# Two routed-mixture stages of a 12-stage kernel: half of the shared expert's work moved from ahead of the row gathers to behind the expert loop

## The chip, the cores and the metric

One core of a Trainium2 chip runs the whole kernel in one launch. The metric is the device time of that launch in microseconds (us), the median over several runs; smaller is better. The engines are TensorE (PE in the profile; PEld are its weight loads), VectorE (DVE), ScalarE (ACT), GpSimd (POOL) and SyncE (SP, which issues most of the DMAs).

## What is computed

Twelve residual stages over 1024 tokens of width 256, `x = x + f(layernorm(x))`, some with a factor of 0.5: routed mixtures, retention, a binarized layer, attention, two kinds of state-space mixers. The change touches the last layer's feed-forward part only, which runs twice, ahead of and behind that layer's mixer (stages 9 and 11 of 0 to 11):

```python
scores = jax.nn.sigmoid(xt @ gate_w.T)                       # 1024 tokens, 8 experts
top_scores, top_idx = jax.lax.top_k(scores, 2)
top_scores = top_scores / (jnp.sum(top_scores, axis=-1, keepdims=True) + 1e-20) * 2.5
combine = jnp.sum(jax.nn.one_hot(top_idx, 8) * top_scores[..., None], axis=1)
h = jnp.einsum('td,edh->eth', xt, w1)                        # d = 256, h = 176
u = jnp.einsum('td,edh->eth', xt, w3)
y = jnp.einsum('eth,ehd->etd', jax.nn.silu(h) * u, w2)
routed = jnp.einsum('etd,te->td', y, combine)
shared = jax.nn.silu(xt @ sw1) * (xt @ sw3) @ sw2            # the shared expert
x = x + 0.5 * (routed + shared)                              # xt = layernorm(x)
```

## The kernel before

The program is written engine by engine. For each stage a planner function makes one list of steps, and every engine's code walks the same list and issues its own part of each step in that order; semaphores do the rest. For these stages the planner is `moe3_order` (L639), and the walkers are `pe_moe3` (TensorE), `a_moe3` (ScalarE), `v_moe3` (VectorE), `g_moe3` (GpSimd) and `sp_moe3` (SyncE). So the list is at once the order of five queues. A step that an engine has nothing to do for is skipped by it.

The steps of the list before, in order:

- `gate`: ScalarE's sigmoid of the eight logits per token (they came from the last `route` step of the stage before, `a_route`), then VectorE picks the two largest (`v_gate3`) and leaves a 0/1 mask.
- `up 0 (0, 1)`, `up 0 (2)`, `up 1 (0, 1, 2)`: the shared expert's gate and up products in plain fp32 (`pe_up3`), half 0 for tokens 0 to 511 and half 1 for tokens 512 to 1023, each in three blocks of rows (0, 1, 2) and each block four matmul records.
- `count`: TensorE counts with a triangular matrix, from the mask, at which place in its expert's list each token stands; VectorE turns the count into one-hot codes (`v_count3`), ScalarE multiplies these by the token numbers (`place`, eight small instructions).
- `table`: eight matmuls make from the codes the table of tokens by expert and place; VectorE spreads it (`v_table3`), and `slots` (two matmuls and a cast) makes the indices for the gathers. GpSimd then gathers the rows of experts 0 to 2 from `Hd`, the normalized tokens in DRAM, 128 rows in one indirect DMA and three of these for an expert (`g_rows3`), and at step `in 0` those of expert 3.
- `swiglu 0`, `swiglu 1`: VectorE multiplies silu and up of each half.
- `split`: ScalarE copies the weights of experts 0 and 1 into rounded high parts (four copies); `low 0` is VectorE's subtraction that leaves the low part of expert 0's gate and up weights. The routed products run as three fp32r passes, high by high, high by low and low by high.
- `overflow`: a branch on all engines that is taken only if an expert has more than 384 tokens; with this input it isn't. Behind it all engines meet at a small DMA (`joined`).
- `down 0` to `down 3`, `sum 0` to `sum 3`: the shared down products, two tiles of 128 tokens each, and their addition to the residual `X` on VectorE.
- the loop over the 8 experts as a software pipeline of three steps, newest first: `in` (transposes of the gathered rows, high and low parts), `mid` (gate, up, silu), `out` (down products, copy, store of the rows to `ye` in DRAM). So a turn is `in e+2`, `mid e+1`, `out e`. `codes` and `weights` compute on VectorE where each token's two results lie and with which weights they count.
- `fetch t 1`, eight times: GpSimd gathers for each tile of 128 tokens the row of the lower of its two experts (0 to 6), which waits until expert 6's rows are stored; then `fetch t 0`, eight times, which waits for expert 7's.
- `add t 1`, then `add t 0` on VectorE: `X` plus weight times fetched row; behind each `add t 0` come the layernorm and transposes for the next stage, or, in stage 11, the store of the output.

The weights of an expert lie in one of five lanes of the buffer `ering` (L2269):

```python
        def lane(e):
            return (0, 1, 2, 3, 4, 0, 1, 2)[e]
```

In stage 9 lane 4 first holds the shared expert's weights, so that expert 4's are loaded behind `down 3`; in stage 11 the shared weights lie elsewhere, and all five lanes are loaded at the start of the stage, in order.

## Time and profile before

| | |
|---|---|
| median of 3 runs | 1900.29 us (1895.18 to 1905.56) |
| the profiled execution | 1914.95 us |
| its span in the profile | 1913.1 us |
| mean granted TensorE clock in it | 0.902 of 2.4 GHz |
| busy: TensorE, VectorE, ScalarE, GpSimd | 83%, 75%, 60%, 47% of the span |
| stage 9 in the trace | about 1088 to 1198 us |
| stage 11 in the trace | about 1803 to 1913 us |

The profile is of one execution; its times are from the span's start. Where two rows carry the same number of matmuls, a plain fp32 matmul counts as two records (it runs in two passes). A row of a timeline merges neighbours of the same kind: `1088.50 5.37 PE ... x8` is eight records that together last 5.37 us. `<-` names what ended the engine's idle time before a row; `remote` and `another core or an unknown queue` stand where no recorded event fits.

### The profile page before, as it was taken

How to read it: one execution, taken by the hardware profiler on the slowest of the kernel's cores; microseconds unless marked ns; L12 is line 12 of the kernel's file. 1: busy time of each engine (PE TensorE's matmuls, PEld its weight loads, DVE VectorE, ACT ScalarE, POOL GpSimd, SP SyncE). 2: the span in 40 equal slices, each digit the busy share in tenths (PEclk: the TensorE clock that was granted, in tenths of full speed). 3: DMA queues.
4: the chain of work that ended last, by engine and by line, in shares of the span. 5: the costliest groups of instructions: out<-in, count | busy, mean ns of one | idle time of the engine just before them, and what ended most of it. 6: DMA issues, size and time to landing. Idle time of an engine off the chain costs nothing.

```text
span 1913.1 us, 28345 instructions
## 1 busy us (share of the span) xinstructions
PE 1585.1 (83%) x10286; PEld 1286.8 (67%) x10286; DVE 1428.8 (75%) x2995; ACT 1154.6 (60%) x2381; POOL 900.9 (47%) x914
## 2 busy tenths in 40 slices
PE   6899468978997276789888975889999999999874
PEld 4799346875996145578567774577777777777573
DVE  6788668657886576777786766778888888888764
ACT  4588146644883137831882243688888888888542
POOL 0677432003775610030252053157787787878353
PEclk9999788988998577979997987899999999999887
DMA  8698310513994200000003042001001000000243
GB/s 306 211 290 261 94 42 25 179 41 98 283 290 148 81 24 1 1 1 1 1 1 115 21 136 95 9 15 34 17 20 31 20 20 28 23 12 15 91 132 108
DMA packets 87449, 158.88 MB, mean 83 GB/s; under 512 B 13560, under 2 KB 62840, under 8 KB 86264
## 3 DMA queue, kind: packets, MB, share of 16 engines
q1 hardware_dynamic: 72696, 116.96, 18.6%
q0 software_dynamic: 14592, 39.87, 7.3%
q8 instruction: 89, 1.46, 0.3%
q14 instruction: 72, 0.59, 0.1%
HBM read 124.28 MB, written 32.51 MB: 82 GB/s over the span
## 4 chain that ended last, share of the span: by engine, by line
PE 29%; DVE 12%; POOL 7%; ACT 4%; issue 3%; DMA 1%; another core or an unknown queue 0%; POOLq 0%; DVEq 0%; ACTq 0%
PE ps L79 26%; POOL work L91 3%; DVE work L91 3%; DVE wt L99 3%; PE ps L83 2%; ACT wt L87 2%; DVE ering L91 2%; POOL work_r L91 1%; ACT L87 1%; DVE X L99 1%; DVE wt L91 1%; POOL wt_r L91 1%; POOL H L145 1%; DVE H L95 1%; ACT work L87 1%
## 5 line engine op out<-in xcount | busy, mean ns | idle before, releaser
L79 PE MATMUL ps<-work_r 128*128 128x256 f32 (+2 forms) x1200 | 243.9, 294 | 8.0 <-DVE work_r L91 3.3
L79 PE MATMUL ps<-wt,work 128*128 128x256 f32 (+1 forms) x1176 | 235.7, 374 | 13.4 <-ACT work L87 8.7
L145 POOL DMA_INDIRECT work<-Hd,work x176 | 169.6, 964 | 137.1 <-DVE work L111 88.9
L79 PE MATMUL ps<-H_r,wt_r 128*128 128x512 f32 x576 | 223.2, 432 | 9.7 <-POOL wt_r L91 7.5
L87 ACT ACTIVATE work<-ps 128x512 f32<-128x512 f32 (+5 forms) x339 | 152.0, 478 | 126.1 <-PE ps L79 59.4
L79 PEld LDWEIGHTS ps<-wt,work 128*128 128x128 f32 (+1 forms) x1176 | 183.1, 203 | 44.2 <-ACT work L87 9.5
L79 PEld LDWEIGHTS ps<-work_r 128*128 128x128 f32 (+1 forms) x1200 | 190.2, 188 | 24.0 <-DVE work_r L91 14.0
L99 DVE SCALAR_TENSOR_TENSOR wt<-ps,wt 128x511 f32<-128x511 f32 (+2 forms) x234 | 174.4, 747 | 22.4 <-ACT wt L87 16.5
L87 ACT ACT_TABLE_LOAD x113 | 145.0, 1283 | 41.3 <-DVE lmv L119 23.5
L91 DVE TENSOR_TENSOR work<-work,ps 48x256 f32<-48x256 f32 (+3 forms) x242 | 128.1, 530 | 50.5 <-PE ps L79 37.5
L91 POOL TENSOR_TENSOR work<-work 128x256 f32<-128x256 f32 (+2 forms) x164 | 162.2, 997 | 6.6 <-ACT work L87 1.3
L91 POOL TENSOR_TENSOR work<-work,wt 128x512 f32<-128x512 f32 x72 | 88.5, 1230 | 133.4 <-DVE work L91 126.5
L79 PEld LDWEIGHTS ps<-H_r,wt_r 128*128 128x128 f32 x576 | 109.3, 190 | 59.1 <-POOL wt_r L91 12.4
L79 PE MATMUL ps<-work_r,ering_r 128*128 128x256 f32 (+3 forms) x480 | 142.6, 297 | 0.0
L79 PE MATMUL ps<-ering,wt 128*64 128x128 f32 (+3 forms) x1488 | 108.7, 286 | 38.7 <-DVE wt L91 25.1
L87 ACT ACTIVATE wt<-wt 128x512 f32<-128x512 f32 (+3 forms) x153 | 132.6, 932 | 5.4 <-DVE wt L91 4.2
L79 PE MATMUL ps<-wt,hT 128*128 128x8 f32 (+4 forms) x384 | 110.3, 432 | 30.1 <-DVE hT L111 14.7
L87 ACT ACTIVATE lrs<-lmv,epsc 128x1 f32<-128x1 f32 x96 | 28.0, 296 | 173.9 <-DVE lmv L119 136.8
L79 PEld LDWEIGHTS ps<-ering,wt 128*64 128x64 f32 (+2 forms) x1488 | 85.1, 137 | 64.8 <-DVE wt L91 27.5
L145 POOL DMA_INDIRECT ering<-ye,get x80 | 78.6, 983 | 104.0 <-DVE X L99 84.3
L91 DVE TENSOR_TENSOR ering<-ering 128x1024 f32<-128x1024 f32 (+4 forms) x88 | 125.8, 1429 | 0.5
L79 PE MATMUL ps<-ering_r,work_r 128*128 128x256 f32 (+1 forms) x398 | 124.5, 348 | 0.4 <-ACT work L87 0.4
(249 smaller groups left out, 4211.3 us busy)
## 6 DMA issues: line engine op xcount, KB each, us to landing
ering<-in_moe_w SPq DMA_DIRECT2D x87, 624.0 KB, 4.9
ye<-work SPq DMA_DIRECT2D x64, 256.0 KB
wt<-in_ssd_wg SPq DMA_DIRECT2D x64, 128.0 KB, 2.2
ye<-work SPq DMA_DIRECT2D x16, 384.0 KB
Hd<-H SPq DMA_DIRECT2D x32, 128.0 KB, 1.7
ye<-early SPq DMA_DIRECT2D x1, 4096.0 KB, 14.6
wt<-in_ssd_wg SPq DMA_DIRECT2D x8, 512.0 KB, 3.6
work<-Hd,work POOLq DMA_INDIRECT x176
```

Of the source, the lines that this page charges most:

```text
L79: self.last = self.e.matmul(o, l, r, start=start, stop=stop, skip_group_check=True)
L83: self.last = self.e.transpose(o, a, ident)
L87: self.last = self.e.activation(o, a, f, **kw)
L91: self.last = self.e.tensor_tensor(o, a, b, op)
L95: self.last = self.e.tensor_scalar(o, a, s1, s2, op0, **(dict(kw, op1=op1) if op1 is not None else kw))
L99: self.last = self.e.scalar_tensor_tensor(out=o, in0=a, scalar=s, in1=b, op0=op0, op1=op1, **kw)
L145: self.last = self.e.indirect_dma_start(out=out, out_offset=at(out_off), in_=in_, in_offset=at(in_off))
```

## The change

It does these things, in the list of steps and what follows from it:

- `split` goes to the front, right behind `gate`; `count` goes ahead of blocks 1 and 2 of `up 0`; `low 0` goes ahead of `table`. `up 1`, `swiglu 1` and all of the `down` and `sum` steps leave the head.
- Behind `overflow` VectorE makes the low parts of expert 0's down and of expert 1's weights.
- The loop is written out: a turn is `in e`, `mid e-1`, `out e-2`. Its end becomes: `down 0`, `out 6`, the eight `fetch t 1`, `mid 7`, `sum 0`, `up 1 (0, 1)`, `out 7`, `up 1 (2)`, `down 1`, `swiglu 1`, the eight `fetch t 0`, `sum 1`, `down 2`, `down 3`, `add` of tiles 0 to 3 from the first fetches, `sum 2`, `sum 3`, `add` of tiles 4 to 7 from the first fetches, then `add t 0` as before.
- ScalarE computes one throw-away sigmoid ahead of the last logits' copy.
- Stage 9 uses four lanes for experts, stage 11 five; the wait for `down 3` and the load behind it are gone. The shared expert's two halves use the same two silu buffers.

```diff
@@ -638,28 +638,25 @@
 
         def moe3_order(si):
             todo, begun, end = [], set(), Steps()
-            todo += [("gate",), ("up", 0, (0, 1)), ("count",), ("up", 0, (2,)), ("place",), ("up", 1, (0, 1, 2)), ("table",)]
-            todo += [("slots",), ("swiglu", 0), ("swiglu", 1), ("split",), ("overflow",), ("low", 0)]
-            todo += [("down", g) for g in range(4)] + [("sum", g) for g in range(4)]
-
-            def expert(e):
+            todo += [("gate",), ("split",), ("up", 0, (0,)), ("count",), ("up", 0, (1, 2)), ("place",), ("low", 0), ("table",)]
+            todo += [("slots",), ("swiglu", 0), ("overflow",)]
+
+            for e in range(8):
                 todo.append(("in", e))
-                if e == 1:
-                    todo.append(("codes",))
-                elif e == 2:
-                    todo.append(("weights",))
-                elif e == 7:
-                    todo.extend(("fetch", t, 1) for t in range(NT))
-                yield
-                todo.append(("mid", e))
-                yield
-                todo.append(("out", e))
-
-            pipeline([expert(e) for e in range(8)], 3, 1, True)
-            for t in range(NT):
-                todo.append(("fetch", t, 0))
-            for t in range(NT):
-                todo.append(("add", t, 1))
+                if e in (1, 2):
+                    todo.append(("codes",) if e == 1 else ("weights",))
+                if e >= 1:
+                    todo.append(("mid", e - 1))
+                if e >= 2:
+                    todo.append(("out", e - 2))
+            todo += [("down", 0), ("out", 6)]
+            todo.extend(("fetch", t, 1) for t in range(NT))
+            todo += [("mid", 7), ("sum", 0), ("up", 1, (0, 1)), ("out", 7), ("up", 1, (2,)), ("down", 1), ("swiglu", 1)]
+            todo.extend(("fetch", t, 0) for t in range(NT))
+            todo += [("sum", 1), ("down", 2), ("down", 3)]
+            todo += [("add", t, 1) for t in range(HALF)]
+            todo += [("sum", 2), ("sum", 3)]
+            todo += [("add", t, 1) for t in range(HALF, NT)]
             for t in range(NT):
                 todo.append(("add", t, 0))
                 end.live.append(after(todo, si, t, begun))
@@ -2091,6 +2088,8 @@
 
         def a_route(a, si, t):
             b = ps.of("route", si, t)
+            if t == NT - 1 and STAGES[si] == "moe3":
+                a.act(lrs[:, 0, 0:1], epsc[:, 0:1], ACT.Sigmoid)
             a.wait_ge(PE, "route", si, t)
             a.act(logits[:, t, :], b.ap[:, 0:8], ACT.Copy).then_inc(A, "logits", si, t).frees(b)
 
@@ -2266,8 +2265,11 @@
                 return SSD["ssd3"].xz.rearrange("p c n -> p (c n)")[:, 0:WP]
             return ering[:, 4, :]
 
-        def lane(e):
-            return (0, 1, 2, 3, 4, 0, 1, 2)[e]
+        def lanes(si):
+            return 5 if STAGES[si - 1] == "ssd3" else 4
+
+        def lane(si, e):
+            return e % lanes(si)
 
         def pe_up3(pe, si, h, blocks):
             wgu, cs = gate_up(shared_weights(si)[:, 0:GU]), slice(h * 512, h * 512 + 512)
@@ -2331,12 +2333,12 @@
                     hi, lo = m.xT[e % 2]
                     pe.wait_ge(V, "xl", si, e)
                     pe.wait_ge(V, "gu", si, e)
-                    w = (m.wgr[e % 2], ering[:, lane(e), 0:GU])
+                    w = (m.wgr[e % 2], ering[:, lane(si, e), 0:GU])
                     pe_swiglu(pe, (si, e), gate_up(w), lambda c, cs: (hi[:, c, :], lo[:, c, :]), slice(0, MAIN3))
                     pe.mark("up", si, e)
                 elif s[0] == "out":
                     e = s[1]
-                    w = down_rows((m.wdr[e % 3], ering[:, lane(e), GU:WP]))
+                    w = down_rows((m.wdr[e % 3], ering[:, lane(si, e), GU:WP]))
                     for j in range(NB):
                         if j % 2 == 0:
                             b = ps.take(pe, "y", si, e, j // 2)
@@ -2350,16 +2352,16 @@
 
         def a_weights3(a, si, e, part):
             h, cut = (M5.wgr[e % 2], slice(0, GU)) if part == "gu" else (M5.wdr[e % 3], slice(GU, WP))
-            a.wait_ge(esem[lane(e)], si, e)
+            a.wait_ge(esem[lane(si, e)], si, e)
             if part == "gu" and e >= 2:
                 a.wait_ge(PE, "up", si, e - 2)
             if part == "dn" and e >= 3:
                 a.wait_ge(PE, "out", si, e - 3)
-            a.act(rnd(h), ering[:, lane(e), cut], ACT.Copy).then_inc(A, part, si, e)
+            a.act(rnd(h), ering[:, lane(si, e), cut], ACT.Copy).then_inc(A, part, si, e)
 
         def low_weights3(q, si, e, part):
             h, cut = (M5.wgr[e % 2], slice(0, GU)) if part == "gu" else (M5.wdr[e % 3], slice(GU, WP))
-            w = ering[:, lane(e), cut]
+            w = ering[:, lane(si, e), cut]
             q.wait_ge(A, part, si, e)
             q.tt(rnd(w), w, f32(h), ALU.subtract).then_inc(q.done, part, si, e)
 
@@ -2378,7 +2380,9 @@
                         a.act(x, x, ACT.Copy, scale=m.ids[:, t:t + 1]).then_inc(A, "numbered", si, t)
                 elif s[0] == "up" and s[2][-1] == 2:
                     h = s[1]
-                    a_swiglu(a, (si, 8, h), m.sg[2 * h], m.sg[2 * h + 1], 512)
+                    if h:
+                        a.wait_ge(V, "sw", 0, si, 6)
+                    a_swiglu(a, (si, 8, h), m.sg[0], m.sg[1], 512)
                 elif s[0] == "split":
                     for e in range(2):
                         a_weights3(a, si, e, "gu")
@@ -2403,8 +2407,8 @@
                     hi, lo = m.aT[e % 2]
                     if e >= 2:
                         a.wait_ge(V, "sw", 0, si, e - 2)
-                    else:
-                        a.wait_ge(V, "sw", 0, si, 8, e)
+                    elif e == 0:
+                        a.wait_ge(V, "sw", 0, si, 8, 0)
                     a_swiglu(a, (si, e), m.sg[2 * e % 4], m.sg[(2 * e + 1) % 4], MAIN3)
                     a.wait_ge(V, "sw", 1, si, e)
                     a.act(rnd(hi[0:48, 1, :]), lo[0:48, 1, :], ACT.Copy).then_inc(A, "ah", 1, si, e)
@@ -2524,7 +2528,7 @@
                 elif s[0] == "swiglu":
                     h = s[1]
                     v.wait_ge(G, "zero rows", si)
-                    v_swiglu(v, (si, 8, h), m.aD, slice(h * 512, h * 512 + 512), m.sg[2 * h], m.sg[2 * h + 1])
+                    v_swiglu(v, (si, 8, h), m.aD, slice(h * 512, h * 512 + 512), m.sg[0], m.sg[1])
                 elif s[0] == "sum":
                     g = s[1]
                     b = ps.of("down", si, 8, g)
@@ -2541,6 +2545,8 @@
                     v.mark("routed", si)
                     v_overflow3(v, si)
                     v.wait_ge(s_join, "in", si)
+                    for e, part in ((0, "dn"), (1, "gu"), (1, "dn")):
+                        low_weights3(v, si, e, part)
                 elif s[0] == "codes":
                     v_codes3(v, si)
                 elif s[0] == "weights":
@@ -2548,16 +2554,13 @@
                 elif s[0] == "in":
                     e = s[1]
                     hi, lo = m.xT[e % 2]
-                    if e:
+                    if e >= 2:
                         low_weights3(v, si, e, "gu")
-                    if e >= 2:
                         v.wait_ge(PE, "up", si, e - 2)
                     for c in range(2):
                         b = ps.of("x", si, e, c)
                         v.wait_ge(A, "xh", si, e, c)
                         v.tt(rnd(lo[:, c, :]), b.ap[:, 0:MAIN3], f32(hi[:, c, :]), ALU.subtract).then_inc(V, "xl", si, e).frees(b)
-                    if e < 2:
-                        low_weights3(v, si, e, "dn")
                 elif s[0] == "mid":
                     e = s[1]
                     hi, lo = m.aT[e % 2]
@@ -2737,7 +2740,7 @@
             if e == 8:
                 sp.dma(shared_weights(si), D["moe3_w"][8]).then_inc(s_shared3, si, by=16)
             else:
-                sp.dma(ering[:, lane(e), :], D["moe3_w"][e]).then_inc(esem[lane(e)], si, e, by=16)
+                sp.dma(ering[:, lane(si, e), :], D["moe3_w"][e]).then_inc(esem[lane(si, e)], si, e, by=16)
 
         def sp_moe3(sp, si):
             m = M5
@@ -2766,14 +2769,11 @@
                 if s[0] == "overflow":
                     sp_overflow3(sp, si)
                     sp.dma(joined, zero[0:1, 0:1]).then_inc(s_join, "in", si, by=16)
-                    if before:
-                        sp.wait_ge(PE, "down", si, 8, 3)
-                        sp_expert3(sp, si, 4)
                 elif s[0] == "out":
                     e = s[1]
-                    if e + 5 < 8:
+                    if e + lanes(si) < 8:
                         sp.wait_ge(PE, "out", si, e)
-                        sp_expert3(sp, si, e + 5)
+                        sp_expert3(sp, si, e + lanes(si))
                     sp.wait_ge(V if e % 2 else A, "y", si, e)
                     rows = ye[e * ROOM:e * ROOM + MAIN3, :].rearrange("(j p) d -> p j d", p=128)
                     sp.dma(rows, m.yo[e % 2]).then_inc(s_ye[e % 2], "out", si, e, by=16)
```

## Rows read from the trace of the kernel before

**Rows 1.** Windows of stages 9 and 11: busy us (count) per engine, granted clock, DMA share, GB/s.
```profile
1104.45:1123.21 18.76, 10.94 (x45) 9.12 (x45) 7.45 (x16) 1.63 (x4) 12.53 (x14) 0.81 0.36 94
1123.21:1168.60 45.39, 45.30 (x300) 44.74 (x300) 38.12 (x81) 31.24 (x66) 17.50 (x17) 0.97 0.46 147
...
1820.20:1839.01 18.81, 11.19 (x45) 9.27 (x45) 7.42 (x16) 1.63 (x4) 12.52 (x14) 0.82 0.32 87
...
1884.60:1909.38 24.78, 0.01 (x1) 0.00 (x0) 8.29 (x18) 0.00 (x0) 15.18 (x16) 0.55 0.49 143
```

**Rows 2.** Timeline of stage 9's head: start us, us, instruction xcount [idle before <-releaser].
```profile
1088.47 1.28 ACT L87 ACT_TABLE_LOAD   x1
...
1088.50 5.37 PE L79 MATMUL ps<-hT,ering 128*128 128x512 f32 x8 [0.32 <-PE ps L79]
...
1089.76 0.26 ACT L87 ACTIVATE work<-logits 128x64 f32<-128x64 f32 x1
...
1092.22 0.30 DVE L95 TENSOR_SCALAR work<-work 128x64 bf16<-128x64 f32 x2
...
1093.70 0.55 PE L79 MATMUL ps<-work,triB 128*128 128x64 bf16 x16
...
1096.43 2.46 ACT L87 ACTIVATE work<-work 128x128 f16<-128x128 f16 x8 [1.94 <-DVE work L91]
...
1099.03 0.15 DVE L111 CAST over<-most 128x1 uint32<-128x1 f32 x1
...
1102.14 0.42 DVE L91 TENSOR_TENSOR work<-ps,work 128x256 f32<-128x256 f32 x1 [2.95 <-PE ps L79]
```

**Rows 3.** Timeline of stage 9's first gathers and shared down products.
```profile
1104.45 0.99 POOL L145 DMA_INDIRECT work<-Hd,work  x1 [14.19 <-DVE work L111]
...
1107.45 0.92 DVE L91 TENSOR_TENSOR ering_r<-ering,wt_r 128x736 fp32r<-128x736 f32 x1 [0.39 <-issue]
1107.47 9.63 PE L79 MATMUL ps<-ering,work 128*128 128x256 f32 x32 [3.50 <-DVE work L91]
...
1118.29 0.95 POOL L145 DMA_INDIRECT work<-Hd,work  x1 [0.31 <-issue]
```

**Rows 4.** Chain that ended last, in stage 9's head: start us, us, what.
```profile
1116.16 5.28 another core or an unknown queue
```

**Rows 5.** DMA of 1104.4 to 1113.3 us: gathers' queue, packets, MB, share.
```profile
q0 software_dynamic: 288, 0.79, 31.2%
```

**Rows 6.** Timeline of stage 11's head.
```profile
1815.79 2.55 ACT L87 ACTIVATE wt_r<-ering 128x736 fp32r<-128x736 f32 x4
...
1823.79 9.88 PE L79 MATMUL ps<-wt,work 128*128 128x256 f32 x32 [4.08 <-DVE ering_r L91]
...
1837.27 0.76 DVE L99 SCALAR_TENSOR_TENSOR X<-ps,X 128x256 f32<-128x256 f32 x2 [4.21 <-remote]
```

**Rows 7.** DMA of 1803 to 1808.9 us: queue of the weights, packets, MB, share.
```profile
q1 hardware_dynamic: 481, 1.56, 74.9%
```

**Rows 8.** Timeline of stage 9's tail.
```profile
1161.36 0.51 PE L79 MATMUL ps<-work_r,wt_r 128*128 128x384 f32 x2
...
1164.50 0.28 PE L79 MATMUL ps<-wt_r 128*128 128x256 f32 x1
...
1170.18 0.96 POOL L145 DMA_INDIRECT H<-ye,get  x1 [9.89 <-DMA ye<-work]
...
1183.00 0.48 DVE L99 SCALAR_TENSOR_TENSOR X<-work,wk,X 128x256 f32<-128x256 f32 x1 [0.77 <-DMA work<-ye,get]
```

**Rows 9.** Timeline behind the last expert of stage 0.
```profile
195.23 3.62 PE L79 MATMUL ps<-ering,wt 128*128 128x256 f32 x16
...
198.68 5.31 PE L79 MATMUL ps<-hT,ering 128*128 128x512 f32 x12
...
211.97 0.59 ACT L87 ACTIVATE work<-ps 48x512 f32<-48x512 f32 x1 [3.67 <-remote]
```

**Rows 10.** Timeline of GpSimd where gathers run beside VectorE's subtractions.
```profile
1124.31 1.13 POOL L145 DMA_INDIRECT work<-Hd,work  x1 [0.30 <-issue]
```

## Prediction

> **What bounds the kernel now.** First the windows, because the shares of a 1913 us span say nothing of a change that touches two of twelve stages. Stage 9 and stage 11 (the routed mixtures of the last layer) have the same four stretches, and two of them leave TensorE idle [rows 1]. From the first row gather to the first routed matmul it works 10.94 of 18.76 us in stage 9 (11.19 of 18.81 in stage 11); through the experts 45.30 of 45.39; behind the last expert 0.01 of 24.78 in stage 11. So the stage is: a head that leads to the gathers' indices, a run of gathers, a loop that TensorE bounds, and a tail that waits for GpSimd's gathers and VectorE's additions. Only head and tail can give.
>
> Then the head in order of time [rows 2]. The sigmoid of the gate waits for its table (load of 1.28 us, sigmoid 0.01 us behind it). TensorE meanwhile runs eight fp32 matmuls, at 0.67 us each, up to 1093.87; only then comes the count, though the mask was there by 1092.5. VectorE's table starts 8.44 us behind the count's start, the first gather 2.31 us behind that.
>
> Then the run of gathers [rows 3]: twelve, one each 1.25 us, from 1104.45 to 1118.29. The shared down products (9.63 us) run beside them and end at 1117.10. But their last sum has to wait: the chain that ended last has 5.28 us of "another core or an unknown queue" from 1116.16 to 1121.44 ahead of it [rows 4]. Stage 11 repeats it, 4.21 us of idle ahead of the same sum [rows 6]. Counted from the end of the down records this is 4.34 us in stage 9 and, with down records that end at 1833.67, 3.6 us in stage 11. 1121.44 is also 3.15 us behind the last gather's issue: either a plain wait, or TensorE's results come late while gathers run. This is the open question of the case.
>
> **The change, part by part.**
>
> *Sigmoid table ahead.* The dummy sigmoid stands before the last logits' copy, where ScalarE was idle, so the mask comes 1.28 us sooner, at 1091.2 [rows 2]. The Trainium skill (ScalarE: Activation LUTs, What ACT_TABLE_LOAD costs) adds a drain of about 1.38 us to each load; by that the step would bring 1.4 us more. The row shows the sigmoid right behind the load, so I don't count it.
>
> *Count behind one block.* Four of the eight matmuls now lie ahead of it: 1088.50 + half of 5.37, rounded up to 3.44 because the first ones run at the half clock (0.86 each) = 1091.94 instead of 1093.70. Gain 1.76; the mask no longer holds it.
>
> *Second up half away from the table.* Between count and table stood 16 matmuls, now 8, and the table waits for ScalarE's numbering instead. VectorE's work behind the count is about 5.5 us, then the low part of expert 0's weights (0.92 to 0.98 us [rows 3]), so the table starts near 1091.94 + 5.5 + 0.98 = 1098.4 instead of 1102.14: −3.7 us in stage 9. In stage 11 the four weight copies (0.64 us each [rows 6]), now ahead of the silus and the numbering, need expert 1's weights. Two experts and the shared constants, 1.56 MB, have arrived only at 1808.9 [rows 7]. From there: copies of expert 1, 1.3, plus the second of expert 0, 0.64; silu's table load 1.28; two silus at 0.59 [rows 9] and numbering 2.46 [rows 2]; together 6.9 with the gaps, so the table starts near 1815.9 to 1816.1 instead of 1817.89 (2.31 ahead of the first gather at 1820.20 [rows 1]): −1.85 us. If those weights come 1.5 us later, nearly nothing is left of this one.
>
> *Gathers to the first expert.* The first routed up product waits for experts 0's and 1's rows, because expert 1's transposes stand ahead of it on TensorE. Six gathers (0.79 MB) had landed 8.85 us behind the first issue [rows 5]. Six transposes (0.12 each), copy, subtraction and hand-overs make 10.3 us from first gather to first routed matmul. Before it was 18.76 and 18.81 in the profile [rows 1]; without the unnamed 4.34 and 3.6 us it would be 14.4 and 15.2. So the gain is 8.4 us in both (8.46, 8.51) if the unnamed stall is in timed runs too, and 4.1 and 4.9 us if it is not. The same 10.3 rests on TensorE's results coming promptly beside the rest of the gathers; if they come only once the twelfth has landed, the gain is nought. These are the two bounds. I take the lower gain, 4.1 and 4.9, since the profiled execution (1914.95 us, span 1913.1) lies 14.7 us above the median of the timed runs, and a stall of this kind, repeated in stages 0, 2, 9 and 11, could be part of that.
>
> *Clock.* TensorE now idles longer ahead of the first expert, and restarts at 1.2 GHz: 0.86 us instead of 0.43 for four or so large matmuls is 1.7 us; before also restarted after some idling. Between 0 and 1.7, I take +0.8 in each stage.
>
> *VectorE beside gathers.* Three subtractions (0.92 each) replace idling, and hold nothing: the first expert's rows land 8.85 us behind. Where gathers met such work they took 1.13 us, against 0.95 [rows 10]: under 1 us for all three, left in the range. The Trainium skill (SBUF — State Buffer, Who interferes with whom) has a VectorE instruction with two SBUF inputs exclude GpSimd's reads for its whole length. By that each gather could start 0.9 later, 2.8 us in a stage, 5.5 in all, and the time would be about 1891.
>
> *Expert loads.* Four lanes instead of five in stage 9: expert 4's 0.64 MB load behind expert 0's end, in less than the 5.9 us that 1.56 MB took [rows 7], and are split an expert's 5.66 us (45.30 / 8 [rows 1]) or more later. Hidden, at most +0.3. SyncE's queue loses a wait and gains none. The overflow branch keeps its place beside the gathers.
>
> *Tail* [rows 8]. Expert 7's up products (1161.36 to 1164.50, 3.14) now stand behind expert 6's end, and one down group ahead of it: a group is 8 of the 16 matmuls that take 3.62 [rows 9], so 1.81. Expert 6's rows are ready 3.14 − 1.81 = 1.33 us sooner, and so are all gathers of the tail. Expert 7 then ends at 1161.36 + 1.81 + 2.05 + 3.14 + 3.54 (8 up matmuls at 0.44) + 2.05 = 1173.95; copy and store take, as for expert 6, about 3.8 us: 1177.8, against 1168.85 + 8 × 1.255 = 1178.9 where its first gather stands in GpSimd's queue. Slack 1.1 us. The rest (4 up, 3 down groups: 1.77 + 5.43) ends at 1181.2; its sum and four additions (0.76 + 4 × 0.48) end at 1183.9, where the final additions started at 1183.00. So stage 9, which VectorE ends, gains nothing here (bounds: −1.3, +0.9); stage 11, which the last gather ends, gains 1.3.
>
> **The sum.** Stage 9: −3.7 −4.1 +0.8 = −7.0. Stage 11: −1.85 −4.9 +0.8 −1.3 = −7.25. Together −14.3 us; from the median, 1886.
>
> **Rivals.**
>
> *The stall is real and goes too.* 8.4 instead of 4.1 and 4.9: −22 us, 1878. For it: the chain shows the stall twice. Against: the profiled run's own height. Chance 0.22.
>
> *TensorE's results come at half speed beside gathers, and the tail pays.* Stage 0 has the new tail's pattern: 16 down matmuls of records 3.62 us, then 12 up matmuls (5.31) beside gathers; the results of the first 24, 7.2 us of records (3.62 and eight at 0.44), were in ScalarE's hands only 16.7 us after the first began [rows 9]: a factor of 2.3, or near 2.2 where gathers pause. Applied behind 1168.85: expert 7's remaining 5.1 become 11.2, its first gather starts at 1183.9 instead of 1178.9; the 7.2 behind it end near 1194, and the final additions start near 1197: +14 in stage 9. Stage 11 ends at 1197 + 8 × 0.48 on stage 9's scale, against 1193.4: +7.5. Head gains with the stall real: −3.7 −8.4 −1.85 −8.5 +1.6 = −20.9. Net +0.6: 1901, or 1893 to 1907. Against: the same sums of the head, in time up to 1116.16 [rows 4]. Chance 0.24.
>
> *Slower: results are held until the run of gathers has landed, head and tail.* The place is the hand-over behind TensorE. The head then gains only the earlier first gather (−5.6), since the first expert again waits for the twelfth. The tail: expert 7 held until 1168.85 + 8.8 + 3.15 = 1180.8, its gathers from 1184.6 on, the down groups held until these have landed, 1196.6; with sums and additions the final additions start at 1200, +17, and stage 11 ends at 1204 against 1193.4, +10.5. Net +22: 1922. It decides as soon as the tail's delay beats the head's gain by 9.5 us, that is from final additions 9 us late upward. For it: 1121.44 and 211.97 both look like it. Against: in stage 9 the chain's down matmuls and sums up to 1116.16 run on without a wait while gathers run. Chance 0.12.
>
> *No effect, because GpSimd's 1.25 us per gather or VectorE's chain bounds both ends anyway.* The head's windows speak against it; 0.02.
>
> **How the numbers follow.** 0.5% is 9.5 us, about what a measurement of this kernel can tell from no change. My forecast (1886, from 1881 to 1892) has 0.40. Faster: 0.40 + 0.22 = 0.62; same 0.24 + 0.02 = 0.26; slower 0.12. The range takes in the forecast, the half-speed rival and most of the real-stall one: 1874 to 1906; it leaves out 1922 and the low edge of 1878.
>
> **What would show it.** In the new profile: first gather 3.7 and 1.85 us sooner from the gate's logits; 10 to 11 us from it to the first routed matmul; expert 7's rows stored before the eighth gather is issued, so that the 16 gathers run at 1.25 us without a gap; final additions within 1 us of their old distance to the loop's end. Wrong if the first routed matmul still waits for the twelfth gather, if a gap opens behind the eighth of the tail's gathers, or if the last shared sums stand behind the last gather.

## The result, and the profile after

The changed kernel takes 1907.27 us (median of 7 runs, 1905.79 to 1911.42) against 1901.38 us (7 runs) of the kernel before on the same chip: ratio 1.003, 95% interval 1.0018 to 1.0042. That is 6 us slower, where 1886 (1874 to 1906) was forecast. Two later comparisons of the same kernel gave 1.0032 (1.0020 to 1.0044) and 1.0025 (1.0011 to 1.0038).

The page of the changed kernel, its span, the first line of busy times and the granted clock in 40 slices:

```profile
span 1905.9 us, 28348 instructions
...
PE 1584.8 (83%) x10286; PEld 1287.7 (68%) x10286; DVE 1428.8 (75%) x2995; ACT 1153.4 (61%) x2383; POOL 900.1 (47%) x914
...
PEclk9999789989998588978988887899999999999778
```

The span is 7.2 us shorter than before's, the opposite of what the timed runs say. The gate's last logits of stage 9 stand at 1073.95 instead of 1088.22, and only the throw-away sigmoid stands ahead of them: the profiled execution of the kernel before lost 14.3 us in the first nine stages that its timed runs mostly don't lose. Stages 0 to 8 are the same in both kernels, and the traces of the changed kernel's other variants have these logits at 1072.7 to 1082.4. So from here on times are counted from the last logits of each stage (1073.95 and 1795.60 after, 1088.22 and 1802.83 before):

| from the last logits, us | before, stage 9 | after | before, stage 11 | after |
|---|---|---|---|---|
| first gather | 16.23 | 12.42 | 17.37 | 16.45 |
| first routed matmul | 34.99 | 23.67 | 36.18 | 27.55 |
| expert 0's second down product (the first with a low part) | 43.49 | 38.54 | 44.89 | 41.23 |
| first of the first fetches | 81.96 | 76.95 | 83.36 | 80.89 |
| first final addition | 94.78 | 101.66 | 96.12 | 104.26 |
| end of the last one | 107.32 | 112.84 | 106.55 | 107.51 |

The head gains and the tail loses more: stage 10 begins 6.9 us later relative to stage 9's logits (its offset to before shrinks from 14.3 to 7.4 us), stage 11 comes out even, together +7 in the traces, +6 in the timed runs.

The windows of the same stretches of stage 9 (columns as in [rows 1]): first gather to first routed matmul, to expert 0's down products, the loop, first fetch to first final addition; then the first three of stage 11:

```profile
1086.37:1097.62 11.25, 2.71 (x12) 2.34 (x13) 4.39 (x7) 1.24 (x3) 8.81 (x9) 0.50 0.33 93
1097.62:1112.14 14.52, 9.10 (x44) 8.67 (x43) 4.71 (x18) 3.51 (x8) 8.71 (x10) 0.74 0.38 95
1112.14:1150.90 38.76, 38.76 (x253) 38.13 (x254) 30.12 (x58) 26.49 (x58) 12.45 (x12) 0.96 0.49 158
1150.90:1175.61 24.71, 11.55 (x50) 8.01 (x48) 9.61 (x23) 3.05 (x5) 15.37 (x16) 0.82 0.34 101
...
1812.05:1823.16 11.11, 2.71 (x13) 2.34 (x13) 4.30 (x7) 1.24 (x3) 8.67 (x9) 0.50 0.33 88
1823.16:1836.49 13.33, 8.23 (x45) 7.88 (x43) 4.72 (x18) 3.46 (x7) 8.91 (x10) 0.88 0.42 106
1836.49:1876.49 40.00, 40.00 (x253) 39.37 (x254) 30.68 (x58) 26.67 (x58) 12.45 (x12) 0.92 0.44 138
```

TensorE works 9.10 of the 14.52 us behind the first routed matmul, where the forecast had the loop running; and 11.55 us between first fetch and first final addition, where before it had next to nothing (0.01 us in the whole tail of stage 11 [rows 1]). The timeline of stage 9's head, which answers to [rows 2] and [rows 3]:

```profile
1074.21 0.26 ACT L87 ACTIVATE work<-logits 128x64 f32<-128x64 f32 x1
...
1077.49 0.68 PE L79 MATMUL ps<-work,triB 128*128 128x64 bf16 x16
...
1083.85 0.42 DVE L91 TENSOR_TENSOR work<-ps,work 128x256 f32<-128x256 f32 x1
...
1086.37 0.99 POOL L145 DMA_INDIRECT work<-Hd,work  x1 [10.38 <-DVE work L111]
...
1093.15 0.94 POOL L145 DMA_INDIRECT work<-Hd,work  x1 [0.30 <-issue]
...
1096.43 1.54 PE L83 MATMUL ps<-cst,work 128*128 128x128 f32 x6 [2.33 <-DMA work<-Hd,work]
...
1097.62 0.99 PE L79 MATMUL ps<-work_r,wt_r 128*128 128x384 f32 x2
...
1103.20 0.48 ACT L87 ACTIVATE work<-ps 48x384 f32<-48x384 f32 x1 [2.72 <-PE ps L79]
...
1108.12 0.95 POOL L145 DMA_INDIRECT work<-Hd,work  x1 [0.30 <-issue]
1110.26 0.56 DVE L91 TENSOR_TENSOR wt<-work,ps 128x384 f32<-128x384 f32 x1 [5.99 <-remote]
...
1112.14 0.55 PE L79 MATMUL ps<-wt_r 128*128 128x256 f32 x1 [5.42 <-ACT wt_r L87]
```

Sigmoid, count and table come as forecast, and the first gather 3.8 us sooner. Expert 1's transposes wait for the sixth gather (issued 1093.15) until 1096.43. Then expert 0's up products run from 1097.62; the second of their three blocks is ScalarE's at 1103.20, but the third, whose record ends at 1102.93, is in VectorE's hands only at 1110.26, 7.3 us later, with 5.99 us of "remote". That is 2.1 us behind the issue of the last of 18 gathers. TensorE stands idle for 5.42 us behind that. The tail:

```profile
1150.90 0.96 POOL L145 DMA_INDIRECT H<-ye,get  x1 [8.42 <-DVE wt L91]
...
1157.11 5.34 PE L79 MATMUL ps<-ering,work 128*128 128x256 f32 x24
...
1159.34 0.76 DVE L99 SCALAR_TENSOR_TENSOR X<-ps,X 128x256 f32<-128x256 f32 x2 [1.34 <-PE ps L79]
...
1165.68 0.76 DVE L99 SCALAR_TENSOR_TENSOR X<-ps,X 128x256 f32<-128x256 f32 x2 [4.00 <-remote]
...
1169.90 0.94 POOL L145 DMA_INDIRECT work<-ye,get  x1 [0.30 <-issue]
1173.36 0.76 DVE L99 SCALAR_TENSOR_TENSOR X<-ps,X 128x256 f32<-128x256 f32 x2 [6.93 <-remote]
...
1175.61 0.48 DVE L99 SCALAR_TENSOR_TENSOR X<-work,wk,X 128x256 f32<-128x256 f32 x1
```

The first fetch comes at 1150.90; 24 records of down groups 1 to 3 end by 1162.45, a third of them for each sum. The first sum is there 0.4 us behind its third, the second (due 1160.7) 5 us late, the last (due 1162.5) 11 us late, at 1173.36: 3.5 us behind the issue of the last gather; in [rows 3, 4] of before it was 3.15. Everything on VectorE, final additions first, waits for these two, and the chain that ended last says so:

```profile
1161.68 3.98 another core or an unknown queue
...
1166.43 6.90 another core or an unknown queue
```

What was late can be told from the trace, which keeps the time of every semaphore update beside the instructions. TensorE's semaphore, for which these sums wait, goes up at 1165.65 and 1173.34, 0.02 to 0.03 us ahead of them: so the delay lies ahead of the signal, not with VectorE. It isn't the loading of code either: the DMA view of 1161.1 to 1173.4 us shows packets of the gathers' queue alone.

### The profile page after: what moved, and what is told of

It is laid out like the page before. It is cut to its first block, busy times and chain, and to the rows that moved or that the text cites. A ratio compares the mean times of both kernels' runs of the same rounds, so it can differ in the third digit from the quotient of the medians.

```text
span 1905.9 us, 28348 instructions
## 1 busy us (share of the span) xinstructions
PE 1584.8 (83%) x10286; PEld 1287.7 (68%) x10286; DVE 1428.8 (75%) x2995; ACT 1153.4 (61%) x2383; POOL 900.1 (47%) x914
## 4 chain that ended last, share of the span: by engine, by line
PE 29%; DVE 12%; POOL 6%; ACT 4%; issue 4%; another core or an unknown queue 1%; DMA 1%; DVEq 0%; SPq 0%; ACTq 0%; POOLq 0%
PE ps L79 26%; POOL work L91 3%; DVE work L91 3%; DVE wt L99 3%; PE ps L83 2%; ACT wt L87 2%; DVE ering L91 2%; POOL work_r L91 1%; DVE X L99 1%; ACT L87 1%; POOL wt_r L91 1%; DVE wt L91 1%; DVE H L95 1%; ACT ering L87 0%
## 5 line engine op out<-in xcount | busy, mean ns | idle before, releaser
L79 PE MATMUL ps<-H_r,wt_r 128*128 128x512 f32 x576 | 224.6, 435 | 11.3 <-POOL wt_r L91 7.4
L83 PE MATMUL ps<-cst,work 128*128 128x128 f32 (+1 forms) x468 | 76.7, 294 | 61.2 <-DMA work<-Hd,work 28.8
L79 PEld LDWEIGHTS ps<-ering,wt 128*64 128x64 f32 (+2 forms) x1488 | 85.4, 137 | 59.2 <-DVE wt L91 23.4
```

What stands on the lines that cost most here:

```text
L79: self.last = self.e.matmul(o, l, r, start=start, stop=stop, skip_group_check=True)
L83: self.last = self.e.transpose(o, a, ident)
```

## The experiments

Twelve kernels, and four repeats (two of them of the changed kernel itself). All but one are edits of the changed kernel; that of 12 and 14 is the kernel before. Ratios are against the kernel before on the same chip.

**1. No second fetch.** In `g_moe3` and `v_moe3`:

```diff
                 elif s[0] == "fetch":
                     _, t, i = s
                     g.wait_ge(V, "get", si)
+                    if not i:
+                        continue
...
-                        v.wait_ge(s_gb[t], "in", si, t)
...
-                    v.stt(X[:, t, :], H[:, t, :] if i else m.gb[t], wk[:, t, i:i + 1], X[:, t, :], ALU.mult, ALU.add)
+                    v.stt(X[:, t, :], H[:, t, :], wk[:, t, i:i + 1], X[:, t, :], ALU.mult, ALU.add)
```

> The changed kernel without the eight second fetches of stages 9 and 11 (each token's result of its higher expert is left out; the first fetch's row is added twice, so the additions on VectorE stay). In the changed kernel the last two shared sums of stage 9 start at 1165.68 and 1173.36, though the down matmuls' records end at 1162.45. Theory A (TensorE's results are handed over late while a run of gathers is in flight): without the second eight gathers both sums start within 1 us of their records, the last by about 1163.5 on the changed kernel's scale. Theory B (the down matmuls themselves are slow at this place, whatever GpSimd does): the last sum still stands 8 to 11 us behind its record.

```profile
1160.17 0.96 POOL L145 DMA_INDIRECT H<-ye,get  x1 [9.20 <-DVE wt L91]
...
1166.37 5.34 PE L79 MATMUL ps<-ering,work 128*128 128x256 f32 x24
...
1168.79 0.76 DVE L99 SCALAR_TENSOR_TENSOR X<-ps,X 128x256 f32<-128x256 f32 x2 [1.53 <-PE ps L79]
...
1171.68 1.42 DVE L99 SCALAR_TENSOR_TENSOR X<-ps,X 128x256 f32<-128x256 f32 x4 [0.55 <-remote]
```

The 24 down records end at 1171.71; the last two sums are the four rows from 1171.68 on, the last of them 0.7 us behind its record. The one before it is still 1.7 us late (record until 1169.99, signal at 1171.66), behind the first eight gathers alone. Nothing on TensorE was changed, so the delays of 5 and 11 us are there because of the second eight gathers. Theory B is out.

**2. A pause in the head's gathers.** In `g_rows3`:

```diff
-            if e >= 4:
-                g.wait_ge(PE, "x", si, e - 4, 1)
+            if e >= 3:
+                g.wait_ge(PE, "up", si, e - 3)
```

> The changed kernel, but the rows of expert e (from 3 on) are gathered only once expert e-3's up products are handed over, so that the head's run is nine gathers and then pauses. Theory A: expert 0's third up block (record 1102.6) is in VectorE's hands within 1.5 us instead of 7.3, the first down product of the loop starts near 1107.5 instead of 1112.1 in stage 9 and 4 to 5 us sooner in stage 11 too; about 9 us off the changed kernel's 1907, so 1898. Theory B: no change, 1907, or slower where a row comes late for its expert.

```profile
1103.12 0.94 POOL L145 DMA_INDIRECT work<-Hd,work  x1 [0.30 <-issue]
...
1108.86 1.15 DVE L91 TENSOR_TENSOR wt<-work,ps 48x384 f32<-48x384 f32 x2 [1.90 <-ACT work L87]
...
1110.13 1.28 POOL L145 DMA_INDIRECT work<-Hd,work  x1 [6.07 <-PE ps L83]
```

Ratio 1.0009 (0.9992 to 1.0026), some 4 us better than the changed kernel's, where 9 were expected. Expert 0's last block is VectorE's at 1108.86, with no "remote", before the gathers resume at 1110.13; the down product of the table stands 32.97 us behind the logits instead of 38.54 (35.89 instead of 41.23 in stage 11). Half of that in stage 9, a third in stage 11, is lost again up to the first fetch (74.28, 77.36), since rows of experts 3 to 6 now come late: TensorE's transposes wait 1.59, 0.48, 1.06 and 0.34 us for them. The tail, which this edit leaves alone, is as late as in the changed kernel (last sum 22.8 us behind the first fetch in both stages).

**3. Final additions of half the tiles ahead of the late sums.**

```diff
-            todo += [("sum", 2), ("sum", 3)]
-            todo += [("add", t, 1) for t in range(HALF, NT)]
             for t in range(NT):
+                if t == HALF:
+                    todo += [("sum", 2), ("sum", 3)]
+                    todo += [("add", u, 1) for u in range(HALF, NT)]
                 todo.append(("add", t, 0))
```

> The changed kernel, but VectorE finishes tiles 0 to 3 (both additions, norm) ahead of the last two shared sums, which only tiles 4 to 7 need. TensorE and GpSimd are as in the changed kernel. If the whole loss of the tail is VectorE standing before these two sums: the final additions of stage 9 start near 1164 instead of 1175.6, and half of them (7.5 us) are done by 1173.4, so 7 us off stage 9 and about 1.6 off stage 11: 1898 to 1899. If the tail's loss is elsewhere (gathers, TensorE's transposes), under 2 us.

Ratio 1.0031 (1.0019 to 1.0042): a miss. The final additions did start 92.2 us behind the logits instead of 101.7, but the next wait on a result of TensorE took the sums' place:

```profile
1177.64 0.69 PE L83 MATMUL ps<-cst,H 128*128 128x128 f32 x2 [1.02 <-DVE X L99]
...
1183.88 0.42 DVE L111 COPY hT<-ps 128x256 f32<-128x256 f32 x1 [5.37 <-remote]
```

Two 128x128 transposes for the next stage are recorded at 1177.64, VectorE's copy of them starts at 1183.88. But this doesn't show that so small a result is held by itself. The down products of the two late sums stand ahead of the transposes on TensorE, their records end at 1170.74 and 1172.46, and TensorE's semaphore goes up at 1182.30 and 1183.77 for them and at 1183.81 and 1183.86 for the two tiles' transposes: the signals came in order, and the small ones stood behind the held ones.

**4. Second up half behind expert 1's up products**, in TensorE's 5 us of idling, with `down 1` and `down 2` ahead of `out 7` and `down 3` behind it:

```diff
+                if e == 2:
+                    todo += [("up", 1, (0, 1, 2)), ("swiglu", 1)]
                 if e >= 2:
                     todo.append(("out", e - 2))
...
-            todo += [("mid", 7), ("sum", 0), ("up", 1, (0, 1)), ("out", 7), ("up", 1, (2,)), ("down", 1), ("swiglu", 1)]
+            todo += [("mid", 7), ("sum", 0), ("down", 1), ("down", 2), ("out", 7), ("down", 3)]
```

> The changed kernel, but the second up half stands behind expert 1's up products, where TensorE idles 5.2 us, with its silu and product; down 1 and down 2 stand behind expert 7's up products, down 3 behind its down products. TensorE's work in the tail is then 5.3 us shorter and all down groups but the last lie ahead of the second fetches. Theory A: all sums are there by the time the third second fetch lands; final additions of stage 9 near 1164 instead of 1175.6 (11 us off), stage 11 ends with its last gather (3 us off): near 1893. Theory B or a factor of 2.2 for all work beside gathers: last sum near 1167, 7 us off stage 9, 2 off stage 11: 1898.

Ratio 1.0001 (0.9988 to 1.0013), short of the forecast. The sums are there 5.3, 7.6 and 10.0 us behind the first fetch, and the final additions start at +91.6, 10 us sooner, in stage 9. But the loop starts later (expert 0's down products at +40.1 and +44.0): it seems that the up half ran in a stretch whose results were held anyway, and made it longer; this was not tested by itself.

**5. Plain DMAs in place of the second fetch**, eight of 128 KB on SyncE's queue:

> The changed kernel with the eight second fetches replaced by eight plain DMAs of the same 128 KB each on SyncE's queue (fixed rows of the store, so the additions get other rows; GpSimd issues nothing there). If what holds TensorE's results is DMA traffic into SBUF at this time: the last two shared sums still stand 4 and 10 us behind their records. If it is GpSimd's gathers as such (theory A as it stands): both within 1 us, as without any second fetch (8.6, 12.2 us behind the first of the first fetches, against 22.4 in the changed kernel).

The last two sums stand 11.3 and 12.0 us behind the first fetch, as in experiment 1 (11.5 and 12.2). The eight DMAs were issued from 1159.92 to 1163.58 and down groups 2 and 3 ran from about 1159.9 to 1163.4, so they met; but the DMAs are over sooner than a run of gathers, and this speaks against DMA traffic as such, no more. The wrong rows unbalance stage 11's routing, and its overflow branch runs: that makes the 2368 us.

**6. The second up half in the head's idle stretch, and a pause.** Order as in 4, but:

```diff
-            todo += [("slots",), ("swiglu", 0), ("overflow",)]
+            todo += [("slots",), ("up", 1, (0, 1, 2)), ("swiglu", 0), ("swiglu", 1), ("overflow",)]
...
+            if e in (3, 4):
+                g.wait_ge(PE, "up", si, e - 3)
```

> The changed kernel with three edits: the second up half with its silu and product runs behind the slots, where TensorE waits 6.7 us for the first rows; the rows of experts 3 and 4 are gathered only once experts 0's and 1's up products are handed over; down 1 and down 2 stand behind expert 7's up products and down 3 behind its down products. From the gate's last logits in stage 9: first routed matmul +26 (the changed kernel has 23.7), expert 0's down products +34.5 (38.5), first of the first fetches +73 (77), final additions from +86 (101.7), last +101 (before: +107.3). In stage 11 last addition +101 (before: +106.5). Together 11 us under the kernel before: ratio 0.994. Theory B (work in the tail slow as such): no better than 1.000.

```profile
1087.66 5.40 PE L79 MATMUL ps<-hT,ering 128*128 128x512 f32 x12
...
1088.32 0.99 POOL L145 DMA_INDIRECT work<-Hd,work  x1 [10.26 <-DVE work L111]
...
1149.08 0.96 POOL L145 DMA_INDIRECT H<-ye,get  x1 [8.36 <-DVE wt L91]
...
1157.54 0.76 DVE L99 SCALAR_TENSOR_TENSOR X<-ps,X 128x256 f32<-128x256 f32 x2 [0.34 <-remote]
...
1162.15 0.48 DVE L99 SCALAR_TENSOR_TENSOR X<-work,wk,X 128x256 f32<-128x256 f32 x1 [0.79 <-DMA work<-ye,get]
```

1886.30 us, ratio 0.9923 (0.9906 to 0.9941); again on another chip 0.9929 (0.9916 to 0.9943). The twelve up records fit between slots and first rows. The last sum is there 8.5 us behind the first fetch, and the final additions follow the gathers, 13.1 us behind it. From the logits: first fetch +73.07, last addition ended +98.56 and +98.38. In the repeat the last additions ended at +101.34 and +98.71. It has the lowest ratio of all the kernels tried.

**7, 9. Its parts.** Experiment 7 is 4 with the pause for experts 3 and 4, experiment 9 is 6 without it.

> Experiment 4 (second up half behind expert 1's up products) and the later gathers of experts 3 and 4 together. The held result goes (5.6 us sooner), but TensorE then has no idle stretch for the up half, which costs its own 5.3 us: expert 0's down products at +38, first fetch +76.7, last addition of stage 9 +104.5, of stage 11 +103.5. 5 to 6 us under the kernel before: ratio 0.997.

> Experiment 6 without its held gathers: second up half behind the slots, down groups 1 to 3 around expert 7's down products, all gathers as early as in the changed kernel. If the two edits are worth what they show one by one: the held result of expert 0's third up block comes back, expert 0's down products at +38.5 to +40 instead of +32.5, and everything behind it 5 to 7 us later in each stage: final additions of stage 9 from +92, ratio 1.000 (between 0.998 and 1.001). If experiment 6 lives from the up half and the order of the tail alone: 0.993 again.

0.9948 (0.9930 to 0.9966) and 0.9954 (0.9935 to 0.9972): 7 better than expected (0.997), 9 between its two theories. In 9 expert 0's down products start at +37.6 and +42.6 instead of +32.5 and +35.8: the pause is worth some 0.3% on top of the placement (the intervals of 6 and 9, from different chips, touch), the placement 0.8% against the changed kernel.

**8. Only the head's part**: shared expert whole ahead of the loop, tail as before.

> Only the head's part of the change: sigmoid table, count, split and low parts as in the changed kernel, but the second up half behind the slots and all down groups and sums ahead of the loop; the tail is expert 7's up, expert 6's and 7's down products as before. If the tail's part of the change is what costs: the stage 9 loss of 5.5 us at its last addition turns into a gain of about 3, stage 11 gains 1 to 2; ratio 0.998. If the down groups in the head cost as much there (7.2 us ahead of the first expert, nothing absorbed by the held results): 1.001 to 1.003.

0.9984 (0.9965 to 1.0004). Stage 9's last addition ended at +103.2 (before 107.3), stage 11's at +105.1 (106.5). The interval takes in 1, so the timed runs don't show a gain over the kernel before; they do show one over the changed kernel. With no work of TensorE in the tail the final additions start 12.8 and 12.9 us behind the first fetch, against 24.7 and 23.4 in the changed kernel. This points, with experiment 1, to the tail's part of the change, which puts TensorE's results beside the fetches, as what makes it slower. The head here is not quite the changed one, since the second up half and the down groups are still in it.

**10, 11. What of the gathers holds the results.** In 10 the second fetch moves 32 of 128 rows in each instruction; in 11 four memsets on GpSimd stand ahead of each.

```diff
-                        g.gather(m.gb[t], None, ye[0:8 * ROOM, :], get[:, t, 0:1]).then_inc(s_gb[t], "in", si, t, by=16)
+                        g.gather(m.gb[t][0:32, :], None, ye[0:8 * ROOM, :], get[0:32, t, 0:1]).then_inc(s_gb[t], "in", si, t, by=16)
```

```diff
+                    if not i:
+                        g.wait_ge(PE, "x", si, 7, 1)
+                        for k in range(4):
+                            g.memset(m.gb[t], 0.0).then_inc(G)
+                            g.wait_ge(G)
```

> The changed kernel with the second fetch gathering 32 of 128 rows in each of its eight instructions, and the additions reading the first fetch's rows as in experiment 1 (each token's result of its higher expert is left out). Same number of gather instructions and the same queue, a quarter of the bytes and packets. If the results are held by the packets or bytes in flight: the last two sums of stage 9 stand 11.5 and 12.2 us behind the first fetch, as without a second fetch. If it is each gather instruction, whatever it moves: 14.8 and 22.4, as in the changed kernel.

```profile
1152.97 0.96 POOL L145 DMA_INDIRECT H<-ye,get  x1 [9.28 <-DVE wt L91]
...
1169.85 0.76 DVE L99 SCALAR_TENSOR_TENSOR X<-ps,X 128x256 f32<-128x256 f32 x2 [6.12 <-remote]
...
1175.47 0.76 DVE L99 SCALAR_TENSOR_TENSOR X<-ps,X 128x256 f32<-128x256 f32 x2 [4.86 <-remote]
```

> The changed kernel with four memsets of the target tile on GpSimd ahead of each second fetch, some 1.3 us together, so that the second eight gathers come one each 2.5 us instead of 1.25. If the results are held because gathers are issued faster than the DMA engines empty their queue: the last two sums move towards their records (under 14 and under 16 us behind the first fetch) although the gathers themselves last 10 us longer. If the results are held as long as any gathers run: the last sum comes some 32 us behind the first fetch, 10 us later than in the changed kernel.

```profile
1156.15 0.96 POOL L145 DMA_INDIRECT H<-ye,get  x1 [8.29 <-DVE wt L91]
...
1168.24 1.51 DVE L99 SCALAR_TENSOR_TENSOR X<-ps,X 128x256 f32<-128x256 f32 x4 [1.25 <-PE ps L79]
```

A quarter of the bytes: in stage 9 the sums are as late as ever, 16.9 and 22.5 us behind the first fetch (14.8 and 22.5 in the changed kernel). In stage 11 they came at 10.4 and 15.9, where the changed kernel has 14.1 and 21.1, and its two repeats 19.7 and 21.2 for the last. So a quarter of the bytes doesn't take the delay away, but in one stage of two it was less: whether bytes have a part in it stays open. With a gather each 2.7 us instead of 1.25: 12.1 and 12.8 us behind, near experiment 1, while gathers go on for another 17 us. The transposes behind them, beside these gathers, are signalled 0.02 us behind their records. So it takes gather instructions in close succession to hold results; the mere presence of gathers doesn't.

**12, 14. A pause in the kernel before.**

```diff
+            if e == 3:
+                g.wait_ge(PE, "down", si, 8, 3)
```

> The kernel before with one wait more: expert 3's three gathers of the head come only once the last shared down group is handed over, so the run is nine gathers and a pause. It settles what the stall ahead of the last shared sum (4.3 and 3.6 us in rows 4 and 6 of the kernel before) is. If it is a result held by the run of gathers, and as real in timed runs as in the profile: the sum comes within 1 us of its record, the first routed matmul 4 and 3.5 us sooner (+31 and +32.7 from the last logits instead of +35.0 and +36.2), ratio 0.996. If it is something else, or is not there in timed runs: ratio 1.000.

> The kernel before with expert 3's gathers behind the last shared down group, as in experiment 12. On a chip with the stall (kernel before at 1901 to 1906): first routed matmul 4 and 3.5 us sooner, ratio 0.996. On one without (1869): 1.000 again.

The two met different chips. On the first the kernel before took 1869.26 us instead of 1901 to 1907, and the pause brought nothing, 0.9999 (0.9990 to 1.0008). On the second (kernel before 1901.09) it brought 0.9972 (0.9960 to 0.9984). The timelines show why. In the whole trace of 12 no idle time ends without a named releaser; in the kernel before's trace VectorE and ScalarE have twelve such waits of over 1.5 us. First stage 0 on the faster chip, then on the slower one, where also stage 9's last shared sum is shown:

```profile
196.21 5.31 PE L79 MATMUL ps<-hT,ering 128*128 128x512 f32 x12
...
199.85 0.59 ACT L87 ACTIVATE work<-ps 48x512 f32<-48x512 f32 x1 [1.12 <-PE ps L79]
```

```profile
197.17 5.31 PE L79 MATMUL ps<-hT,ering 128*128 128x512 f32 x12
...
205.44 0.59 ACT L87 ACTIVATE work<-ps 48x512 f32<-48x512 f32 x1 [4.34 <-remote]
...
1093.41 9.70 PE L79 MATMUL ps<-ering,work 128*128 128x256 f32 x32 [3.50 <-DVE work L91]
...
1103.14 0.75 DVE L99 SCALAR_TENSOR_TENSOR X<-ps,X 128x256 f32<-128x256 f32 x2 [0.97 <-PE ps L79]
```

Same instructions: on the faster chip ScalarE has the second up block 3.6 us behind the start of the twelve records, on the other 8.3 us, and in [rows 9] 13.3. On the slower chip the pause does in stage 9 what was expected: the down records end at 1103.11, the last sum starts at 1103.14, and the first routed matmul stands at +30.96 instead of +34.99. Whether the held results make up all of the 32 us between the chips is not shown.

**13, 15, 16. Repeats** of the changed kernel (1.0032, 1.0025) and of experiment 6 (0.9929), all on chips where the kernel before takes 1901.

> The changed kernel as it is, once more. If this chip is of the kind on which the kernel before takes 1869 us: no stall, the head's and tail's gains as forecast (14 us), ratio 0.992 or 0.993, last addition of stage 9 some 7 us and of stage 11 some 7 us nearer to the gate's logits than in the kernel before. If it is of the kind with 1901 to 1906: 1.003 again.

> Experiment 6 again. On a chip with the stall 0.992 as before. On one without, its held gathers cost nothing and bring nothing, and it keeps the head's earlier gathers, the up half in TensorE's idle stretch and the short tail: 0.990 to 0.993.

> The changed kernel as it is. On a chip without the stall (kernel before near 1869 us): ratio 0.992 or 0.993. On one with it: 1.003.

A chip of the faster kind was not met again, so the changed kernel was never timed on one, and the 0.992 expected there is neither shown nor refuted.

## Why the prediction was wrong

- **Sigmoid table, count, table.** Right in stage 9, half in stage 11. The mask's sigmoid starts at +0.26 us instead of +1.54, the count 3.54 behind the logits (5.48), the first gather 3.8 us sooner (forecast 3.7). The Trainium skill's drain of 1.38 us behind a table load (ScalarE: Activation LUTs, What ACT_TABLE_LOAD costs) is not to be seen here either: the next activation starts 0.01 us behind the load at 1076.94. In stage 11 the first gather is 0.9 us sooner instead of 1.85: the three last weight copies end 8.7 us behind the logits (8.0 forecast), and table and slots matmuls, behind idling, run slower, 2.35 for 1.04 us and 0.62 for 0.40 of before, at granted clocks of 0.77 and 0.50.
- **Gathers to the first expert.** 11.25 and 11.11 us instead of 10.3: expert 1's rows come 3.3 us behind the sixth gather's issue, and the transposes run at the half clock (1.54 us; granted clock 0.50 in this window). A term mis-sized by 0.9.
- **The step that failed first: "The same 10.3 rests on TensorE's results coming promptly".** They came promptly for the first routed matmul and not for what it made. Expert 0's third block was held 7.3 us, beside a run of gathers that in the new order is 18 long and not twelve, so of 11.3 us gained at the first matmul only 4.95 were left at expert 0's down products (3.66 of 8.6 in stage 11). Both bounds of the prediction looked at the first matmul alone. By the table the head was worth 4.95 + 3.66 = 8.6 us; the forecast had 7.0 + 5.95. Its clock term, +0.8 in each stage, looked at the first matmuls alone too: the idling behind them brought a second slow stretch, with expert 0's down products in 3.3 us instead of 1.8.
- **Taking the lower gain because the stall might not be in timed runs.** Wrong reason. The stall is in timed runs on this kind of chip (experiment 14: −0.28%), and the profiled execution's extra 14 us lay ahead of stage 9. That the lower gain is the one nearer to the result is luck.
- **Gathers beside VectorE's subtractions.** Three subtractions ran from 1089.25 to 1091.38, and one gather took 1.43 us instead of 0.95; in stage 11 two took 1.30 and 1.13. That is 0.5 us in each stage, under the 1 us of the forecast. The Trainium skill's exclusion (SBUF — State Buffer, Who interferes with whom), from which the prediction worked out an estimate of 2.8 us a stage, is not borne out at that size.
- **Tail: expert 6's rows.** They were to come 1.33 us sooner than the loop alone gives. First fetch against expert 0's down products: 38.41 against 38.47 in stage 9, 39.66 against 38.47 in stage 11. The gain was eaten by the loop's slow start behind the held stretch, the 3.3 instead of 1.8 us just named; the granted clock is 0.96 and 0.92 in the loop's windows.
- **Tail: expert 7's rows in time.** Right. The second eight gathers follow without a gap (1160.92, and 1.25 us apart but for one).
- **The step that failed worst: "its sum and four additions (0.76 + 4 × 0.48) end at 1183.9", i.e. the last down group handed over as its record ends.** It was 11 us late, and the final additions started 24.7 us behind the first fetch, where the forecast adds up to 15.1 (1183.9 − 1168.85) and the kernel before had 12.8. Less the 5.0 us gained up to the first fetch, that is stage 9's +6.9. Of the three signs of being wrong that the prediction named, this is the third, the last shared sums behind the last gather; the other two did not come.
- **Rivals.** What happened is the mechanism of the "slower" rival, held results in head and tail, at a third of its total: it had +17 and +10.5 in the tail and no gain beyond 5.6 in the head; there were 11.9 in stage 9 (first fetch to final additions) and 3.4 in stage 11 (first fetch to the last one's end), and 8.6 gained. By its number the half-speed rival (1901, up to 1907) is the nearest to 1907.27, but its mechanism is not what happened: the 24 down records keep their pace (5.34 us), and held signals come in bursts, as below. At 1.003 the result is within 0.5% of no change, which had 0.26, while 0.62 lay on faster. The evidence stood in [rows 3, 4, 6, 9], the same unnamed wait, ended about 3 us behind the last gather's issue, and in the tail of the new order it met work of TensorE that the old order didn't have there.

What is held can be read from TensorE's semaphore. In stage 9 of the kernel before, the last shared sum waits for down products that end at 1117.09, and ScalarE and GpSimd wait for transposes that end from 1117.42 to 1118.40. All of them go on together:

```profile
1121.47 0.76 DVE L99 SCALAR_TENSOR_TENSOR X<-ps,X 128x256 f32<-128x256 f32 x2 [5.31 <-remote]
1121.58 0.87 ACT L87 ACTIVATE work_r<-ps 128x384 fp32r<-128x384 f32 x2 [18.98 <-remote]
1121.80 0.95 POOL L145 DMA_INDIRECT work<-Hd,work  x1 [2.57 <-remote]
```

The five updates stand at 1121.44, 1121.49, 1121.54, 1121.60 and 1121.65. With the pause (experiment 14) each of the same five stands 0.01 to 0.02 us behind its record. In the changed kernel's head two transposes and three blocks of expert 1, whose records end from 1103.25 to 1106.72, are signalled from 1111.67 to 1111.94, five updates in 0.27 us, and stage 11 repeats it (1837.42 to 1837.70). A block takes TensorE 1.05 us by the records (1104.63 to 1105.67), so it can't be computed in the 0.08 us between two updates: here TensorE's work was done, and only its signal was late. For the two sums of the tail, whose updates come one by one, this is likely but not shown.

What stays open is what in the chip holds a signal. The runs show that it takes gather instructions some 1.25 us apart (experiments 1, 11), that fewer bytes alone don't cure it (10), that a pause after nine gathers avoids it in the head (2, 6, 14), and that one chip shows none of it (12). It isn't there beside every such run: in the kernel before, transposes at 1185 to 1191 were handed over at once although gathers ran, and in experiment 6 those at 1165 to 1168 too. TensorE had been idle for 16.7 and some 9 us before these, which may matter and was not tried.

## What to carry to other kernels

An idle wait that the profile can't name and that ends again and again at about the end of a run of transfers is to be taken as part of the place, not as noise: price every piece of work that an edit moves beside such a run with that wait, and at its consumer, not at its own start. Where TensorE's results are wanted while GpSimd gathers, put a pause behind some nine gathers (tried in the head only), or move that work ahead of the run; and fill TensorE's idle time with work whose results nobody wants soon. Count two traces from a common instruction just ahead of the change before comparing their spans.

## What the runs showed of the hardware

- Beside gather instructions issued 1.25 us apart TensorE's signals came up to 10.9 us behind the records of its matmuls (1162.45 to 1173.34), in the heads five within 0.21 to 0.28 us. With the second eight 2.7 us apart the two sums' signals were 2.3 and 1.3 us late, against 1.7 and 0.03 with no second eight at all, and later ones 0.02 us.
- The same kernel took 1901 to 1907 us on most chips and 1869 us on one, where no such wait is in the trace of experiment 12. Stage 0's second up block, 3.6 us behind its start there, took 8.3 and 13.3 us on others, in identical code.
- A gather of 32 rows takes GpSimd 0.87 us against 0.95 for 128: nearly all of an issue is fixed.
